# Index masks on ScalarE, a one-row canonical table, a reordered y product and split weight transfers in a four-layer decode kernel

## What is computed

```
L0: y = einsum('bct,bcd->bdt', x, w0[conditions])             # per sequence, 32x32 weights over the 32 tokens
L1: q,k,v = x Wq, x Wk, x Wv ; rms-norm and rope on q and k
    k and v written into paged blocks of 16 tokens, at slots given by block_tables and kv_lens
    scores over the last 128 positions (window), softmax, weighted sum of v, times Wo
L2: base = x W_base ; lora = ((x Wt) A[idx]) B_w[idx] Wp * scaling
L3: y = einsum over the 32 tokens with w3[subjects]
```

## Time and profile before

| | us |
|---|---|
| three runs | 223.39, 221.33, 223.25 (median 223.25) |
| the profiled execution | 220.62 |
| its span, first to last instruction | 218.4 |
| start to about 20 | loads, rope table, first index operations |
| 20 to 73 | phase 1 |
| 73 to 98 | between the phases, first scores |
| 98 to 218 | phase 2, 7.1 to 7.5 per tile, and the last three steps |

### The profile page before, as it was taken

One profiled execution on the slowest core, in us unless ns is written; L12 is line 12 of the kernel. 1 busy time (PEld: TensorE's weight loads), 2 busy tenths in 40 slices (PEclk: granted clock), 3 DMA queues, 4 the chain that ended last, 5 costly groups with the idle time before them and its releaser, 6 DMA issues.

```text
span 218.4 us, 6833 instructions
## 1 busy us (share of the span) xinstructions
PE 188.2 (86%) x2361; PEld 146.0 (67%) x2361; DVE 183.7 (84%) x468; ACT 124.4 (57%) x462; POOL 82.4 (38%) x103
## 2 busy tenths in 40 slices
PE   0466999799999895288899999999999999999882
PEld 0453555476666683277787788888888888888660
DVE  4668998899987898279999999999999899999740
ACT  5032634233445638059866876798778967795510
POOL 5303004004765385733463355336533644320010
PEclk9999999999999999569999999999999999999998
DMA  3479999960213241534523453455435435521111
GB/s 91 145 169 267 252 211 307 297 200 29 98 68 97 83 139 51 153 107 134 165 74 103 146 166 90 135 168 171 99 139 166 146 99 159 158 66 29 29 51 48
DMA packets 20769, 28.95 MB, mean 133 GB/s; under 512 B 10637, under 2 KB 16024, under 8 KB 20354
## 3 DMA queue, kind: packets, MB, share of 16 engines
q0 software_dynamic: 6928, 18.00, 28.2%
q1 hardware_dynamic: 12962, 9.63, 15.8%
q10 hardware_dynamic: 848, 0.92, 1.5%
HBM read 28.31 MB, written 7.64 MB: 165 GB/s over the span
## 4 chain that ended last, share of the span: by engine, by line
PE 66%; DVE 14%; DMA 7%; issue 5%; ACT 3%; POOL 2%; ACTq 1%; POOLq 0%; DVEq 0%
PE bank L1229 15%; PE quad L1243 12%; PE quad L1194 9%; PE bank L1269 6%; PE bank L1283 4%; PE bank L1225 4%; PE quad L1264 4%; PE bank L1257 3%; PE bank L1276 3%; DMA merged<-qT,idx 2%; PE bank L1181 2%; DMA yall<-in_w,scratch 2%; DMA big<-merged,idx 2%; PE quad L1167 2%; DVE onT L1042 2%
## 5 line engine op out<-in xcount | busy, mean ns | idle before, releaser
L727 ACT ACTIVATE work<-bank,nmx 128x164 f32<-128x164 f32 x128 | 49.9, 408 | 33.2 <-DVE nmx L1025 33.1
L1229 PE MATMUL bank<-kt_rope,big 128*128 128x164 f32 x256 | 45.6, 313 | 0.0
L1229 PEld LDWEIGHTS bank<-kt_rope,big 128*128 128x128 f32 x256 | 41.8, 199 | 4.0
L580 POOL DMA_INDIRECT big<-merged,idx x16 | 16.5, 1032 | 46.7 <-DMA big<-in_pool,idx 25.5
L1035 DVE STREAM_TRANSPOSE work<-work 128x768 f32<-128x768 f32 (+1 forms) x64 | 32.7, 548 | 0.0
L1194 PE MATMUL quad<-wqkv_sb,yall 128*128 128x512 f32 x64 | 30.7, 602 | 0.3 <-ACT yall L675 0.3
L1025 DVE TENSOR_REDUCE nmx<-bank 128x3 f32<-128x492 f32 (+1 forms) x48 | 28.4, 591 | 1.8 <-PE bank L1229 1.3
L727 ACT ACTIVATION_READ_ACCUMULATOR work<-bank,nmx 128x1 f32 x128 | 27.6, 215 | 0.0
L706 ACT ACTIVATE big<-qT,con 128x256 f32<-128x256 f32 x64 | 27.2, 500 | 0.0
L551 POOL DMA_INDIRECT merged<-qT,idx x16 | 18.0, 1124 | 23.3 <-DVEq L929 13.4
L1042 DVE TENSOR_TENSOR onT<-quad,rT 32x256 f32<-32x256 f32 (+1 forms) x48 | 19.9, 415 | 6.0 <-PE quad L1243 4.8
(11 more groups left out here) (154 smaller groups left out, 325.8 us busy)
## 6 DMA issues: line engine op xcount, KB each, us to landing
xin<-in_x SPq DMA_DIRECT2D x16, 128.0 KB, 4.3
merged<-big SPq DMA_DIRECT2D x2, 1024.0 KB, 8.6
out<-x4s SPq DMA_DIRECT2D x16, 128.0 KB, 1.8
merged<-own SPq DMA_DIRECT2D x1, 1024.0 KB, 10.1
w3bd<-w_scratch SPq DMA_DIRECT2D x64, 4.0 KB
wqkv_sb<-in_wqkv ACTq DMA_DIRECT2D x1, 512.0 KB, 3.8
w_scratch<-yall SPq DMA_DIRECT2D x1, 256.0 KB, 3.5
wt_sb<-in_wt SPq DMA_DIRECT2D x1, 256.0 KB
```

What stands on the lines that cost most here:

```text
L727: act.activation(prob[:, p, hd, 0:NK], ps_sc[(p + i) % 2][:, j * NK:j * NK + NK], ACT.Exp, bias=nmx[:, p, hd:hd + 1], scale=1.0, accum_out ...
L1229: mm = pe.matmul(at[:, j * NK:j * NK + NK], qbd[:, p, hd, :], kT[:, p, hd // GSZ, 0:NK], start=False, stop=(j == n - 1), skip_group_check= ...
```

## The change

Line numbers below are those of the kernel before. It is one bundle of seven edits.

1. **Masks.** DVE's two operations over all tiles go; ACT writes the mask of each tile with two Relu activations (128 and 36 columns), four of them at the end of each of its steps 12 to 19. The mask's value is now a positive distance and not 1, and the product with -1e30 still removes the position. ACT's phase 1 has 20 steps as before, but the last three hold masks and roots only.
2. **Canonical row.** `canonical` writes one partition instead of 64. ACT copies the row of 704 to SBUF in its step 8 (two copies of 352), PE turns it into 64 x 11 by 11 matmuls with one row and one column (`by_batch`, in step 9, ahead of `outward`), and DVE copies 64 x 11. The four DVE operations of L875 and L878 go. `lists_of_rows` and `shifted_lists` move from behind DVE's step 4 to behind step 5, `rows_of_tiles` from 6 to 7.
3. **Order of y.** Of the 24 items 7 stand inside phase 1 (0 to 3 in step 9, then one in each of 12, 14, 16), 14 after it, and the last 3 (z7, a7, b7: `RAMP`) inside phase 2's first step, between the second and the third group of scores.
4. **Transfers.** The blocks of tile 1 for two of the four sequences go from ACT's queue to POOL's; the transfers for tiles 2 to 15 are split into tiles 2 to 5 (two on SP, two on ACT) and tiles 6 to 15 (four on SP).
5. **Gathers.** `cached` 0 and 1 are issued after the scatters of tiles 9 and 11 (before: 10 and 13), `cached` 2 right after the last scatter and before the wait for them to land (before: after tile 1's merged rows). The pads are cleared by DVE.
6. **Rope.** The sum is one operation of 384 columns with a step of -192 over the two halves of the second operand, not two of 192. The rope table is built behind the small index operations, not ahead of them.
7. **Lags.** For tiles 10 to 15 ACT's root and DVE's normalised row come one step earlier.

```diff
-        ps_canon = [bank[5][0:B, 0:HALF], bank[6][0:B, 0:HALF]]
+        ps_canon = [bank[5][0:1, 0:HALF], bank[6][0:1, 0:HALF]]
...
+        AGAIN = 6
+        LAG = 10
+        ROOTS = {s: tuple(t for t in range(NT) if s == t + (4 if t < LAG else 3)) for s in range(NT + 4)}
+        ROWS = {s: tuple(t for t in range(NT) if s == t + (2 if t < LAG else 1)) for s in range(NT + 2)}
-        INLINE.update({9: ITEMS[0:4]})
-        INLINE.update({s: ITEMS[s - 7:s - 6] for s in range(11, NT + 2)})
-        AFTERWARDS = ITEMS[NT - 5:]
+        INLINE.update({9: ITEMS[0:4], 12: ITEMS[4:5], 14: ITEMS[5:6], 16: ITEMS[6:7]})
+        AFTERWARDS = ITEMS[7:-3]
+        RAMP = ITEMS[-3:]
... SP
             sp.wait_ge(s_w0d, 16)
+            for b in range(2):
+                dst, src = blocks_of(b, SOON, AGAIN)
+                sp.dma_start(dst, src).then_inc(s_w0[SOON], 16)
             for b in range(NB):
+                dst, src = blocks_of(b, AGAIN, NT)
+                sp.dma_start(dst, src).then_inc(s_w0[SOON + 1], 16)
... POOL
+            for b in range(2, NB):
+                dst, src = block_of(b, 1)
+                pl.dma_start(dst, src).then_inc(s_w0p, 16)
...
                 scattered(t)
-                if t in (10, 13):
-                    cached((t - 10) // 3, (t - 10) // 3)
-            wait(krow_done, NT)
+                if t in (9, 11):
+                    cached((t - 9) // 2, (t - 9) // 2)
+            cached(2, 2)
             for t in range(NT):
                 wait(s_scat[t], 16)
-            for p in range(2):
-                pl.memset(prob[:, p, :, NK:KW], 0.0).then_inc(s_pad, 1)
... ACT
+            def masks(t):
+                for k, (name, a, b, sign) in enumerate((("backpos", 0, NKB, -1.0), ("ownpos", NKB, NK, 1.0))):
+                    act.activation(mask[:, t, a:b], cc(name), ACT.Relu, bias=pos3[:, k, t:t + 1], scale=sign
+                                   ).then_inc(mask_done, 1)
...
+                if s == 8:
+                    act.wait_ge(s_ipe, 2)
+                    for part_of_blocks in range(2):
+                        act.copy(canon_row[:, HALF * part_of_blocks:HALF * part_of_blocks + HALF],
+                                 ps_canon[part_of_blocks]).then_inc(s_canoned, 1)
...
+                if 12 <= s < 12 + PAIRS:
+                    if s == 12:
+                        act.wait_ge(s_rows, 1)
+                        act.wait_ge(s_conm, 16)
+                    for t in (2 * (s - 12), 2 * (s - 12) + 1):
+                        masks(t)
... DVE
-                ve.wait_ge(s_ipe, 2)
-                for part_of_blocks in range(2):
...
+                ve.wait_ge(s_ipe, 3)
+                link(ve.tensor_copy(canon, ps_idx[0:B, 400:400 + SPAN]))
...
-            AFTER = {0: (same_blocks,), 2: (segments,), 4: (lists_of_rows, shifted_lists), 6: (rows_of_tiles,)}
+            AFTER = {0: (same_blocks,), 2: (segments,), 5: (lists_of_rows, shifted_lists), 7: (rows_of_tiles,)}
...
-                    for a in range(2):
-                        ve.tensor_tensor(turned[:, a], straight[:, a], crossed[:, 1 - a], ALU.add).then_inc(rsum_done, 1)
+                    crossed = bass.AP(crossed.tensor, crossed.offset, [crossed.ap[0], (-192, 2), (half, 12), (1, half)])
+                    ve.tensor_tensor(turned, straight, crossed, ALU.add).then_inc(rsum_done, 1)
... PE
+            def by_batch():
+                pe.wait_ge(s_canoned, 2)
+                for i in range(SPAN):
+                    mm = pe.matmul(ps_idx[0:B, 400 + i:401 + i], canon_row.rearrange("p (b i) -> p i b", i=SPAN)[:, i],
+                                   ident[0:1, 0:1], start=True, stop=True)
+                mm.then_inc(s_ipe, 1)
...
-            INDEX = {5: (dead_tokens,), 6: (inward,), 8: (canonical,), 9: (outward,), 10: (tiles,)}
+            INDEX = {5: (dead_tokens,), 6: (inward,), 8: (canonical,), 9: (by_batch, outward), 10: (tiles,)}
...
+                if s == 0:
+                    for kind, pair in RAMP:
+                        inputs(kind, pair)
```

More of the change, by code:

```diff
@@ L279, in build @@
         tmp1 = scr(48)
+        canon_row = late[0:1, 128:128 + B * SPAN]
         idxf = more[:, 192:320].rearrange("p (k r) -> p k r", k=4)
@@ L638, in _ @@
             act.dma_start(con[0:B, la:lb], consts[0:B, la:lb]).then_inc(s_conl, 16)
+            act.wait_ge(s_w0d, 16)
+            for b in range(2, NB):
+                dst, src = blocks_of(b, SOON, AGAIN)
+                act.dma_start(dst, src).then_inc(s_w0[SOON], 16)
             act.wait_ge(s_blkd, 16)
@@ L687, in phase1 @@
                     outward()
[L688 to L689 removed]
+                for t in ROOTS[s]:
                     act.wait_ge(ss_done, t + 1)
@@ L708, in queries @@
                                    ACT.Copy, scale=only).then_inc(qbd_done, 1)
-            for kind, p in AFTERWARDS:
-                if (kind, p) in (("z", PAIRS - 1), ("b", PAIRS - 1)):
-                    if p == PAIRS - 1 and kind == "z":
+            for n, (kind, p) in enumerate(AFTERWARDS):
+                if n >= len(AFTERWARDS) - 2:
+                    if n == len(AFTERWARDS) - 2:
                         act.wait_ge(s_init, 48)
-                    queries(int(kind == "b"), int(kind == "b"))
+                    queries(n - len(AFTERWARDS) + 2, n - len(AFTERWARDS) + 2)
                 copied(kind, p)
@@ L997, in _ @@
                         part_of_index()
+            for p in range(2):
+                ve.memset(prob[:, p, :, NK:KW], 0.0).then_inc(s_pad, 1)
             for t in range(2):
                 normalised(t)
-            for k in range(2):
-                masks(k)
             def keys(t, p, r, n):
@@ L1266, in phase2 @@
                     scores(t, p, 1)
+                if s == 0:
+                    for kind, pair in RAMP:
+                        inputs(kind, pair)
                 if valid(t2):
+                    if t2 == 0:
+                        pe.wait_ge(zx_copied, PAIRS)
                     for c in range(2):
```

104 lines of the change are left out of this document (49 added, 55 removed).

## The result

Twenty runs of the changed kernel have a median of 224.62 us (221.89 to 232.54), beside 222.51 us (220.74 to 226.42) for twenty of the kernel before. The ratio is 1.0062, 95% interval 1.0033 to 1.0091. The forecast was 219.8 us, with 216.2 to 222.6 for 8 in 10. The profiled execution took 224.47 us, with a span of 222.6; the one before took 220.62, with 218.4. That one was faster than all twenty runs of its kernel, so the two profiles lie 3.85 us apart where the ratio says 1.4: what follows explains these two executions, and more than the kernels' difference. Ratios here leave disturbed executions out, medians do not.

What follows compares the result with a forecast made beforehand. Up to about 105 us the chain through POOL's scatters and gathers was taken to bound the kernel, with PE and ACT the new bound. -4.6 + 1.3 for the clock gave -3.3: 217.3 us profiled, 219.8 median, 216.2 to 222.6 for 8 in 10.

Steps and rivals of the forecast that it cites:

- The start: nothing: Edits 4 and 6: DVE reaches tile 0 up to 2 us sooner, but PE waits for tile 8's x anyway; gain 0.
- the pause that I made myself, behind phase 1: PE idle 3.7 us ahead of pair 3's product; a fall to half clock costs 0 to 2.75 us, taken as +1.3.
- the rival with a chance of 0.06: Start of kernel: x of tiles 6 and 7 caught behind the block loads, +2.4 us in all, 225.6 us; chance 0.06.
- about 1 us: SP's queue at the start: two more transfers issued ahead delay x by about 1 us; block loads also begin about 1 later.
- `by_batch`, 1.8 us (1.4 to 2.7): PE's 22 issues behind tile 8's product take 1.8 us; the index chain and first scatter come 2.1 us later.
- The front, added up: PE up to the last Wqkv product: -2.6 + 1.4 = -1.2 us, so the last squares start at 70.1, not 71.3.
- The scatters: POOL, edits 1, 5, 7: -5.4 us; 1.30 us apart from 53.6, last at 75.7, own gather at 78.4.
- The masks: ACT behind the last squares: twelve masks cost 3.1 us less one root of 0.3; pair 3's product starts at 76.4.
- The rival that the stall is not the masks': POOL's 2.83 us scatter comes again though DVE's masks are gone: about 220.6 us; chance 0.08.
- From the last y to `rwide`: Ramp into phase 2: from last y at 86.4 to the copy to `rwide` at 95.7, against 100.27: -4.6 us at full clock.
- Phase 2: nothing: From the copy to `rwide` on, phase 2 is as before: no change.
- The rope sum: DVE in each tile: two operations overlapping to about 0.55 us become one of about 0.5; counted 0, +0.4 a tile if slow.

Runs made afterwards that it cites:

- e8: The kernel before with edit 4 alone (the new transfers): 225.78 us against 222.43, ratio 1.014.
- e4: The changed kernel with edit 1 undone, masks back on DVE: 225.20 us against 222.74 for the kernel before, ratio 1.004.
- f1: Changed kernel, edits 2 and 4 undone, tile 7's product ahead of tile 8's x, pause ahead of pair 3's product filled: 224.27 us, 0.989 to the kernel before.
- e1: The changed kernel with four unread 128x512 products on PE ahead of tile 8's x product: 232.41 us, 1.005 to the kernel before.
- f4: The kernel before with edit 1 alone, masks on ACT: 229.75 us against 227.98, ratio 1.007.
- g2: The changed kernel with edits 1, 2 and 4 undone: 225.48 us against 229.16 for the kernel before, ratio 0.999.
- h2: The changed kernel with edits 1, 2 and 4 undone, run again in another set: 224.07 us against 227.44 for the kernel before, ratio 0.987.
- f3: The kernel before with edit 2 alone, `by_batch` added: 229.41 us against 227.98, ratio 1.013.
- the last three sets: Third to fifth of five sets of follow-up runs, each with its own runs of the kernel before: 228.0, 229.2 and 227.4 us.
- g3: Changed kernel, edit 4 undone, `by_batch` and tile 7's product ahead of tile 8's x, pause ahead of pair 3's product filled: 228.57 us, 1.017 to the kernel before.
- the first two sets: First and second of five sets of follow-up runs, each with its own runs of the kernel before: 222.7 and 222.4 us.

## Why the forecast was wrong, step by step

**The start: nothing.** This step failed first, in the forecast's words "what is early is absorbed there". I let x of tile 8 land at 36.8 whatever happened ahead, and looked at the early start as merely absorbed. It was absorbed, but as 4.06 us of idle PE in front of the index work, and the clock paid for it. I saw the clock only in the pause that I made myself, behind phase 1. In other executions it was the rival with a chance of 0.06, x of tile 6 or 7 caught: seven of the nine profiles with the new transfers. Its mechanism and place were right; its price, 5.7 us on top of the forecast, is more than the 1.4%, 3.1 us, that e8 measures for edit 4 alone. The two more issues that I counted as "about 1 us" are half of what puts x behind the gather. The other half is the gather itself, which starts earlier than before (18.74 against 19.70 us), not later as I held: POOL no longer waits for four transfers of 14 tiles each, but for four of 10 and four of 4, on two queues.

**`by_batch`, 1.8 us (1.4 to 2.7).** It took 2.91 or 2.92 us in all eleven profiles that have it, at full and at half clock: 132 ns for each of 22. I went by L1129 for its equal weights; the row with as little to stream and fp32, L1148 at 0.125, was the nearer one, and even that was short. The Trainium skill ("TensorE: Matmul & The Clock Gate", Back-to-back issue gap) gives about 60 cycles to a single matmul of up to 64 columns, 25 ns at 2.4 GHz, without its weight load; each product here has a new one, the rows show 132 ns, and the measured figure decides. Worse than the size is what I did not see: the clock falls behind it. In nine of the ten profiles in which it began at full clock, the clock was at 0.50 within 2 to 5 us of its start (e4 is the exception). In the eight profiles without it, e8 apart, the clock is 1.00 from 38 to 46 us (in f1 it falls at 47.2, behind a wait of 1.90 us). One rival is untested: edit 2 also makes `canonical` a product with one column of weights, and no run has one without the other. Against it: in e1 5.7 us of larger products lay between the two, and the clock fell 2.2 us behind the start of `by_batch`.

**The front, added up.** The last squares came at 75.57, not 70.1. Of the 5.5 us, about 1.2 is the later x (37.99 against 36.78), 1.1 the size of `by_batch`, 2.6 `outward` at half clock (5.4 against 2.8), and 0.5 tile 8's x product at half clock (1.23 against 0.71).

**The scatters.** The queue behaved as worked out: 18 operations, 57.91 to 82.49, 1.37 us apart where I had 1.30, and no stall, though three scatters took 1.25 to 1.38 us. The own gather came at 84.58 instead of 78.4: 4.3 us of the 6.2 are its start, 1.2 the spacing, 0.7 a longer wait for the last scatters to land.

**The masks.** Twelve of them take 3.05 us (3.1), so pair 3's product starts 6.13 us after the last squares (6.3). The clock falls at the end of the pause (81.8), and costs 1.7 us at pair 3's product (1.3). All that was right. f4 shows the edit alone as a loss of 0.7% all the same, with an interval that starts at 0.1%, and e4 shows no gain from undoing it. That the stall it takes away is worth less than the pause and the slower product that it brings is my reading; no profile shows it. The rival that the stall is not the masks' is refuted. In e4, g2 and h2, with the masks on DVE, a gather of POOL takes 1.97, 2.50 and 2.49 us beside them, in e8 and f3 a scatter 2.82 and 2.83, and in no kernel with the masks on ACT does a scatter take over 1.4. The Trainium skill's sentence that spoke for this rival ("SBUF — State Buffer", Who interferes with whom) is not borne out by these rows.

**From the last y to `rwide`.** 93.4 to 103.05 is 9.7 us, where I had 86.4 to 95.7, 9.3.

**Phase 2: nothing.** I held that from that copy on phase 2 is as before; it took 1.4 us more. The whole: the forecast for a profiled execution was 217.3, and 224.47 came. 6.1 us lie ahead of `rwide` (103.05 against 97, 5.5 of them in the front), 1.4 behind it, and 0.3 comes back because this execution is only 1.9 us longer than its span. The median missed by less, 4.8 us, for the 2.6 us that I added from execution to median were 0.2 in the changed kernel.

**The rope sum and the gathers.** One operation of 384 takes 548 ns, where two of 353 overlapped to 0.62: nothing or a gain of 0.07 us a tile, as counted. The edits left in h2 (3, 5, 6 and 7) are worth 1.3% together in its set, and nothing that can be told in g2.

What stays open is phase 2's length, and stalls of ACT in the last three sets. There, in nine of ten profiles, ACT stands still between 58 and 73 us, for 1.9 to 6.1 us at the longest, and the profile names no semaphore:

```profile
66.11 0.37 ACT L696 COPY yall<-bank 128x256 f32<-128x256 f32 x1 [6.11 <-remote]
```

This row is of g3. No profile of the first two sets has one. It may belong to the 5 us that the kernel before takes longer in these sets, but no profile of that kernel was taken there.

## What to carry to other kernels

Work that starts earlier moves the idle time, and the place where it lands is to be costed like any other pause: ask what stands behind it at half clock. Two more issues on a transfer queue can decide which of two streams goes first; write down the order of issues across all queues, not only within one. Behind a string of tiny products the clock fell in nine of ten profiles: what follows such a string is part of its price. And a single profile of each kernel can differ by more than the kernels do; look at where its time lies before it is taken for the effect.

## What the runs showed of the hardware

- 22 fp32 matmuls with one row of weights, 64 wide, and one column cost 132 ns each at either level of the clock, 2.91 us together, and in nine of ten profiles the granted clock went to half within 2 to 5 us of their start though PE was busy throughout them (e1: no gap from 33.5 us on, 0.50 from 45.2).
- Two transfers of 128 KB took 4.2 us from issue to landing ahead of the block gathers, and 6.5 and 16.0 us when issued 0.3 and 0.8 us behind the first of them (e8); in the changed kernel's profile, issued as late, they took 4.1 and 4.2.
- A DVE operation with two SBUF inputs, 2.9 us for two of 2048 columns, went with one indirect DMA of POOL beside it of 1.97 to 2.83 us, in all six kernels that had the masks there; with the masks on ACT none took over 1.38 us.
